# Two-layer graph network on one core: all four waves of the first-edge search placed inside the sort

## What is computed

```python
edge_index = jnp.stack([src, dst])
x = _layernorm(x + _L0_gnn_ref(x, edge_index, ...))   # sheaf layer: MLP per edge, two reflections,
                                                      # degrees of src and dst, scatter-add to both ends
x = _layernorm(x + _L1_gnn_ref(x, edge_index, ...))   # two GCN convolutions: gather by src,
                                                      # segment_sum over dst, tanh
```

## Time and profile before

| what | us |
|---|---|
| median of 3 runs (lowest 7209.48, highest 7219.2) | 7216.2 |
| the profiled execution, time of its run | 7211.55 |
| its span | 7209.8 |
| VectorE busy in the span | 6251.0 |
| TensorE busy in the span | 4330.9 |
| ScalarE busy in the span | 4847.9 |
| GpSimd busy in the span | 2842.8 |
| first group of the count behind the key gathers starts at | 181.12 |
| last group of the count starts at | 618.71 |
| first compare of the sort starts at | 643.57 |
| first list mark after the sort starts at | 1197.04 |

### The profile page before, as it was taken

The page is one execution under the profiler, slowest core; times in us unless marked ns, Lnnn a source line. Parts: engine busy times, 40 slices in busy tenths (PEclk is TensorE's granted clock), DMA queues, the critical chain, the costliest instruction groups (busy, mean ns, idle before and its releaser), DMA issues.

```text
span 7209.8 us, 242628 instructions
## 1 busy us (share of the span) xinstructions
PE 4330.9 (60%) x83890; PEld 3454.6 (48%) x83890; DVE 6251.0 (87%) x9722; ACT 4847.9 (67%) x13314; POOL 2842.8 (39%) x2217
## 2 busy tenths in 40 slices
PE   1443000277758778777888888666566655567554
PEld 0342000277755555555555555455466544566443
DVE  4679998388878888899999999999977899777998
ACT  1665104044448888888999999899666777566775
POOL 5221303555525555522222222378400388100785
PEclk6666555599988988888988999887765799665998
DMA  4100000288853333333333333344599645899445
GB/s 64 8 8 8 6 0 26 83 320 316 320 208 104 106 106 103 105 102 109 115 117 118 116 115 117 89 121 120 136 366 367 230 120 120 253 365 367 123 121 93
DMA packets 510830, 1043.59 MB, mean 145 GB/s; under 512 B 125764, under 2 KB 316580, under 8 KB 509956
## 3 DMA queue, kind: packets, MB, share of 16 engines
q1 hardware_dynamic: 376932, 760.52, 29.6%
q0 software_dynamic: 113920, 281.72, 16.2%
q10 hardware_dynamic: 19872, 0.11, 0.2%
HBM read 755.92 MB, written 286.18 MB: 145 GB/s over the span
## 4 chain that ended last, share of the span: by engine, by line
issue 23%; DVE 23%; PE 17%; ACT 15%; ACTq 6%; POOL 6%; DVEq 4%; DMA 3%; another core or an unknown queue 2%; SPq 0%; POOLq 0%
PE ps L1171 5%; ACTq L1059 5%; DVE keys L1543 3%; PE ps L1198 3%; PE ps L1291 2%; DMA val_rows<-val_out 2%; POOL got L675 2%; ACT apartb L1012 2%; POOL sw_inb L675 2%; DVE xs_ring L1927 2%; ACT step_lo L778 2%; DVEq L1821 2%; DVE keys L1542 2%; DVE dst_hot L1757 1%
## 5 line engine op out<-in xcount | busy, mean ns | idle before, releaser
L675 POOL DMA_INDIRECT xs_ring<-xd_rows,src_idx x488 | 596.4, 1222 | 1630.3 <-DVE xs_ring L1927 1445.4
L1817 DVE TENSOR_TENSOR wide_hotb<-dst_key,iota_b 128x1792 bf16<-128x1792 bf16 x879 | 950.9, 1082 | 8.1 <-ACT val_out L1070 4.1
L2090 DVE TENSOR_SCALAR wide_hotb<-sw_inb,slot_id 128x2048 bf16<-128x2048 bf16 x976 | 689.1, 750 | 265.8 <-PE ps L1326 264.9
L1326 PE MATMUL ps<-wide_tabb,wide_hotb 128*128 128x48 bf16 x15616 | 659.0, 208 | 315.6 <-ACT wide_tabb L1060 298.8
L675 POOL DMA_INDIRECT got<-val_rows,dst_idx x296 | 391.4, 1322 | 1155.1 <-DMA val_rows<-val_out 1064.3
L1198 PEld LDWEIGHTS ps<-wide_tab,wide_hot 128*128 128x128 bf16 x23424 | 635.2, 98 | 435.6 <-issue 249.7
L1198 PE MATMUL ps<-wide_tab,wide_hot 128*128 128x32 bf16 x23424 | 680.9, 180 | 173.7 <-issue 120.3
L1326 PEld LDWEIGHTS ps<-wide_tabb,wide_hotb 128*128 128x128 bf16 x15616 | 599.1, 113 | 375.8 <-issue 374.5
L1291 PE MATMUL ps<-got,wide_hotb 128*128 128x96 bf16 x7104 | 451.6, 225 | 342.9 <-DVE got L2033 245.4
L1012 ACT ACTIVATE apartb<-iota_b,rel_negb 128x128 bf16<-128x128 bf16 x1758 | 605.4, 391 | 24.4
L1171 PE MATMUL ps<-row_tab,dst_hot 128*128 128x64 bf16 x15744 | 531.5, 193 | 150.2 <-issue 103.4
(11 more groups left out here) (425 smaller groups left out, 12212.6 us busy)
## 6 DMA issues: line engine op xcount, KB each, us to landing
sw_inb<-src_wide SPq DMA_DIRECT2D x488, 512.0 KB, 5.8
xd_rows<-xd_out SPq DMA_DIRECT2D x128, 984.0 KB
sw_in<-src_wide SPq DMA_DIRECT2D x244, 512.0 KB
val_rows<-val_out SPq DMA_DIRECT2D x488, 192.0 KB, 5.0
dw_in<-dst_byte SPq DMA_DIRECT2D x128, 656.0 KB, 4.0
msg_rows<-msg_out SPq DMA_DIRECT2D x244, 200.0 KB
xs_ring<-xd_rows,src_idx POOLq DMA_INDIRECT x488
got<-val_rows,dst_idx POOLq DMA_INDIRECT x296
```

The source lines that it names most:

```text
L675: return pool.indirect_dma_start(out=into, out_offset=None, in_=table, in_offset=bass.IndirectOffsetOnAxis(index, 0))
L1326: last = mm(ps_val[s * 2 + h][:, t, :], wide_hot2[s][:, half, e:e + P], wide_tab2[s][:, h, half * 3 * D:(half + 1) * 3 * D], start=half == ...
L1817: return v.tensor_tensor(to.rearrange("p t (j k) -> p t j k", k=2), rel.unsqueeze(2).to_broadcast(shape), iota_b[:, 0:w].rearrange("p (j k ...
L2090: last = v.tensor_scalar(wide_hot2[q % 2][:, half, :], sw_in2[q][:, :], slot_id[:, half:half + 1], None, ALU.is_equal)
```

## The change

GpSimd issues the key gathers first and then all four waves, behind a wait for the first sort step. VectorE's counting loop is one loop with no probe in it. The four probes stand behind sort steps 18, 36, 54 and 72, and the degrees behind step 74.

```diff
-        COUNTED = (1, 20, 42, GROUPS // 2)
-        WAVES_AT = (6, 48)
+        WAVES_AT = (18, 36, 54, 72)
         STEPS = sum(n + 1 for n in range((WID - 1).bit_length()))
-        assert WAVES_AT[1] + 2 < STEPS
+        assert WAVES_AT[PROBES - 1] + 2 < STEPS
...
-            wave(0)
             pool.wait_ge(seg_ready, 1)
             pool.wait_ge(keys_stored, 16)
             for c in range(COLS):
                 gather(keys[0][:, c * P:(c + 1) * P], key_rows, seg_idx[:, c:c + 1]).then_inc(seg_got, 16)
-            for s in range(1, PROBES):
+            pool.wait_ge(sort_stepped, 1)
+            for s in range(PROBES):
                 wave(s)
...
-            for n in range(3):
-                with dve.Fori(COUNTED[n], COUNTED[n + 1]) as i:
-                    for e in range(2):
-                        dve.wait_ge(hot_free, i * 2 + (e - 1))
-                        one_hots(e, i * (2 * T) + e * T)
-                if n < 2:
-                    probe(n)
+            with dve.Fori(1, GROUPS // 2) as i:
+                for e in range(2):
+                    dve.wait_ge(hot_free, i * 2 + (e - 1))
+                    one_hots(e, i * (2 * T) + e * T)
...
                     if stepped in WAVES_AT:
-                        probe(2 + WAVES_AT.index(stepped))
-                    if stepped == WAVES_AT[1] + 2:
+                        probe(WAVES_AT.index(stepped))
+                    if stepped == WAVES_AT[PROBES - 1] + 2:
                         degrees()
```

## The result

The changed kernel takes 7120.4 us (median of 4 runs, 7120.02 to 7130.42) against 7212.84 us; the ratio is 0.9875, 95% interval 0.9858 to 0.9892. A second comparison on another chip gave 0.9873 (0.9858 to 0.9888). The forecast was 7133 us, range 7103 to 7163. The profiled span fell from 7209.8 to 7118.3 us, by 91.5; the sum had said 83.1.

What follows compares the result with a forecast made beforehand. No engine bounds the whole span; count and sort pass changes on one for one. Head and count -171.8, two added probes +13.8, waits +74.9: -83.1 from the median 7216.2 gives 7133 us, range 7103 to 7163.

Steps and rivals of the forecast that it cites:

- The head: Set-up before the count: without wave 0 ahead of the key gathers, 77 memsets cost 3 us instead of 58.3; -55.3 us.
- The count: Counting loop, eighth to 125th group: without waves 1 and 2 and probes 0 and 1, 437.6 us becomes 321.1; -116.5 us.
- moves but stays: Count under the 41 key gathers: they start earlier but still starve it, so that loss was taken as unchanged.
- The waits: Sort: VectorE stands at the four probes until each wave's remaining gathers land; +74.9 us in all.
- The counting rule: Sort: 0.94 gathers pass beside each VectorE instruction; those left at a probe take 1.29 us each plus 3.5 us.
- landing: End of each wave in the sort: a gather's data is there 3.5 us after the gather's end.
- The rule of the Trainium skill: Sort: compares would let gathers through at full pace, so the 74.9 us of waits would vanish; 4%.
- Queues and later stages: Engine queues and everything behind the sort: nothing is pushed, all at 0; without its cover each 2 us at most.
- rival 1: Sort hides the waves whole, so no waits at the probes: 7058 us; 4%.
- rival 2: Starvation follows the waves into the sort, hitting short instructions: 15 to 35 us lost in all; 15%.
- rival 3: Slower than before: gathers beside the sort at 4.2 us each, waits together over 158 us; 3%.

Runs made afterwards that it cites:

- the repeated run: The changed kernel, unaltered, measured once more on the chip of the last group of runs: 7114.76 us, ratio 0.9873 to the kernel before.

## Why the prediction was right

**The head** was put at -55.3; 56.5 went (58.32 to 1.80). The memsets took 0.02 us each, not 0.04. Putting wave 0 back alone brought the 55 us of idle time back.

**The count** was put at -116.5 from the eighth group to the last; head and count together at -171.8. Measured: -178.5, and -173.3 in the repeated run. The term that was off is the one set to "moves but stays", the key gathers. They let seven groups through in one profile and five in the other, at 1.33 and 1.29 us a gather; two groups are 5.4 us. The rest of the difference is 1.2 us in the head. That ScalarE's pace of 2.76 us would limit the undisturbed count held: the last 80 groups came 2.75 us apart.

**The waits** were put at 25.4, 22.9, 21.6 and 5, sum 74.9. Measured: 24.33, 20.95, 19.99 and 7.58, sum 72.85. The counting rule behind them, 0.94 gathers to one VectorE instruction, had been read as a ratio only. The timelines and the split compares show that a boundary lets at most one through, and that this is the mechanism. Some of the closeness is luck. Not yet through when VectorE stood were 18, 15, 15 and 5 gathers, where the prediction had 17, 15, 14 and 4, but landing was put at 3.5 us and took 1.65 to 2.62 from the last gather's end to the probe. The two errors partly offset each other. The 5 us of the last wave were a choice between 0 and 8.7; it was 7.58.

**The rule of the Trainium skill** (SBUF — State Buffer, "Who interferes with whom"), by which a tensor_tensor was not seen to hold up a DMA, was weighed and given 4%. It doesn't describe this kernel: the f32 compares with both inputs in SBUF hold each gather until the next boundary. The same section says that such a tensor_tensor contends with a GpSimd instruction that reads SBUF. The gather takes its indices from `probe_i`, which lies in SBUF, so that clause could have forecast the wait; which access of the gather is held was not tried. The section also says that the pair is held for a whole instruction. That agrees with gathers that get through only at a boundary, but no run shows the port itself: each gather still lasts 0.8 to 0.9 us into the next compare, and the compare is not longer for it (2.89 us at 465.10, before the first gather, and 2.89 at 513.65, among them).

**Queues and later stages** at 0: the span behind the end of the sort changed by less than 1 us between the two first profiles.

**The rivals.** No waits (rival 1): wrong by 72.85 us. Starvation in the sort (rival 2): no gap "on issue" appeared in it, among the short instructions of the fourth wave either, where gathers came 1.95 us apart. With split compares gathers came even 1.43 us apart there without a gap on VectorE, where the count would have lost 32 to 40 us. Slower (rival 3) needed 4.2 us a gather; they came 1.95 to 2.23 apart with the fast tail in it, and 2.53 to 2.59 beside the long compares. The 3.35 us that the prediction set against this rival was the longer of two gathers shown; the longest of that wave took 5.34. It was the mean of 2.48 that carried the argument.

**What stays open** is what the gathers take from the other engines' issue. Shown: a limit that holds GpSimd back between gathers removes it; the loss was 32 us or more in every burst of the count at 1.45 us a gather or less, and 6 or less in every one at 1.75 or more; it comes with two in flight as well, from either table, and at DMA shares of 0.28 and of 0.09; no instruction loading by DMA is needed; no semaphore holds the waiting matmul of the earlier trace rows. That the sort is spared is put down to its few, long instructions (274 compares of 1344 ns on average even when split, against TensorE's 50 matmuls in two groups of the count), but this was argued and not tried. VectorE's own two comparisons in a group of the count are no longer, 1.35 and 1.42 us, so the length of its instructions alone would not do it; it would have to be the many short ones of TensorE and ScalarE, for which it waits.

## What to carry to other kernels

In this kernel, gathers issued back to back by GpSimd nearly halted the engines that run many short instructions. Look at the pace of the burst, and try holding it back before moving the burst elsewhere: two in flight cost one wait for each gather and gave 39 us for 41 gathers. Check that the limit really makes GpSimd wait; in wave 2 it hardly did. Beside long VectorE compares the same gathers cost nothing (VectorE busy 120.14 of 121 us) but were slow themselves, at most one to an instruction: count boundaries, not microseconds, when you place the wait for them. And a burst that is moved under other work must be given as much of it as the burst needs there, not as it needed where it was.

## What was not expected of the hardware

- At most one gather for each VectorE boundary. All 49 gathers of wave 3 in the kernel before end 0.78 to 0.91 us after an f32 compare has begun; half as long compares took the pace of waves 0 to 2 from 2.53 to 2.59 us beside the sort to 1.43 to 1.71 us.
- Two profiles of the same kernel differ by two groups of the count let through by the 41 key gathers, about 5 us; their gathers came 1.33 and 1.29 us apart. Which of the two is the cause is not shown.
- Gathers of rows of `dst_samples`, a table of 28 KB, kept the DMA engines busier (share 0.28) than those of `dst_blocks` (0.10) at nearly the same pace, and with two in flight came 2.03 us apart against 1.44.
